# The search of the blocks' first edges in five groups, placed beside the adjacency blocks of a graph kernel

## What is computed

```
def spmm(x): return segment_sum(edge_weight[:, None] * x[src], dst, num_segments=n)
acc = cur = x
for _ in range(3):
    cur = spmm(cur); acc = acc + cur
x = layernorm(x + acc)

h = (x @ W_node.T).reshape(n, 4, 32);  e = (edge_attr @ W_edge.T).reshape(E, 4, 32)
att = leaky_relu(sum(concat[h[src], h[dst], e] * a), 0.2)
m = maximum(segment_max(att, dst), 0);  ex = exp(att - m[dst])
denom = segment_sum(ex, dst) + (E - deg) * exp(-m)
x = layernorm(x + segment_sum(ex / denom[dst] * h[src], dst))
```

## Time and profile before

| | |
|---|---|
| median of 3 runs | 1601.72 us (1601.37 to 1603.68) |
| the profiled execution | 1605.02 us, span 1603.3 us |
| PE busy | 1359.4 us, 85% |
| DVE busy | 1004.7 us, 63% |
| ACT busy | 681.5 us, 43% |
| 0 to 81 us | records, searches, counts; 24 attribute chunks |
| 82 to 413 us | the 25 adjacency blocks and 80 chunks |
| 431 to about 880 us | the three layers |
| to 1603 us | scores, attention, last norm |

### The profile page before, as it was taken

The page is one execution under the profiler, slowest core; times in us unless marked ns, Lnnn a source line. Parts: engine busy times, 40 slices in busy tenths (PEclk is TensorE's granted clock), DMA queues, the critical chain, the costliest instruction groups (busy, mean ns, idle before and its releaser), DMA issues.

```text
span 1603.3 us, 49688 instructions
## 1 busy us (share of the span) xinstructions
PE 1359.4 (85%) x22245; PEld 992.1 (62%) x22245; DVE 1004.7 (63%) x1519; ACT 681.5 (43%) x1600; POOL 130.5 (8%) x102
## 2 busy tenths in 40 slices
PE   4969999996499999999997898838888886888885
PEld 3959988886244454454445898825656654566564
DVE  5389999999200010000114898888888887888874
ACT  3236666664110000001111000047777777777776
POOL 1511011100000000000000000021111110111000
PEclk9999999998799999999997999968999998899998
DMA  6628787756779699869971776400000000000000
GB/s 207 222 82 242 220 248 218 233 150 160 229 258 409 228 345 325 300 215 373 301 281 44 201 208 202 136 29 13 13 13 13 13 13 8 12 13 14 26 3 24
DMA packets 214641, 250.30 MB, mean 156 GB/s; under 512 B 43578, under 2 KB 146487, under 8 KB 214294
## 3 DMA queue, kind: packets, MB, share of 16 engines
q1 hardware_dynamic: 210422, 236.52, 45.5%
q0 software_dynamic: 4000, 10.54, 2.1%
HBM read 197.88 MB, written 49.14 MB: 154 GB/s over the span
## 4 chain that ended last, share of the span: by engine, by line
PE 44%; DVE 27%; DVEq 12%; DMA 7%; issue 4%; ACT 4%; SPq 1%; POOL 0%; ACTq 0%; POOLq 0%
PE bank L682 25%; DVE Lq L1351 7%; DVEq L1304 5%; PE bank L609 4%; DVE L L1166 4%; DVE Hx L1358 3%; PE bank L749 3%; DVE Hw L1176 3%; PE bank L719 2%; DVEq L1366 2%; PE bank L579 2%; DVEq L1171 2%; DMA hib<-slp 2%; PE bank L760 2%; DMA drow<-in_dst,rowi 2%
## 5 line engine op out<-in xcount | busy, mean ns | idle before, releaser
L1014 ACT COPY Att<-bank 128x400 f32<-128x400 f32 x800 | 336.7, 525 | 121.7 <-PE bank L749 120.0
L749 PE MATMUL bank<-Hx,Lq 64*128 64x100 f16 x6400 | 229.7, 218 | 96.6 <-DVE Hx L1358 91.0
L749 PEld LDWEIGHTS bank<-Hx,Lq 64*128 64x128 f16 x6400 | 170.6, 100 | 176.8 <-DVE Hx L1358 103.6
L760 PE MATMUL bank<-Att,xa 128*32 128x128 f32 x5000 | 222.2, 295 | 0.0
L609 PE MATMUL bank<-L,Hw 128*52 128x128 bf16 x4800 | 167.9, 225 | 35.6 <-DVE Hw L1176 27.4
L1358 DVE TENSOR_TENSOR Hx<-Hq,wdup 128x3328 f16<-128x3328 f16 x100 | 184.7, 1889 | 3.7
L609 PEld LDWEIGHTS bank<-L,Hw 128*52 128x52 bf16 x4800 | 144.7, 108 | 45.4 <-DVE Hw L1176 38.8
L894 ACT COPY rows<-bank 116x512 f32<-116x512 f32 x200 | 117.8, 589 | 119.3 <-PE bank L609 105.1
L719 PE MATMUL bank<-Tp,lob 128*128 128x100 bf16 x2418 | 152.9, 211 | 15.9 <-DVE sel L1290 13.7
L719 PEld LDWEIGHTS bank<-Tp,lob 128*128 128x128 bf16 x2418 | 148.3, 99 | 19.7 <-DVE sel L1290 11.3
L682 PE MATMUL bank<-pieces,xs 128*128 128x512 f32 (+1 forms) x350 | 137.2, 552 | 17.8 <-DMA pieces<-adj 17.8
(11 more groups left out here) (175 smaller groups left out, 1359.1 us busy)
## 6 DMA issues: line engine op xcount, KB each, us to landing
pieces<-adj SPq DMA_DIRECT2D x90, 1280.0 KB, 8.9
adj<-rows SPq DMA_DIRECT2D x100, 416.0 KB
lob<-slp SPq DMA_DIRECT2D x26, 992.0 KB, 6.3
ea<-in_edge_attr SPq DMA_DIRECT2D x25, 992.0 KB, 8.5
hib<-slp SPq DMA_DIRECT2D x78, 64.0 KB, 4.8
pieces<-adj SPq DMA_DIRECT2D x15, 320.0 KB, 3.1
lh_d<-dup SPq DMA_DIRECT2D x25, 64.0 KB, 4.3
lhd<-lh_d SPq DMA_DIRECT2D x25, 64.0 KB, 1.8
```

The costliest lines, as they stand in the source:

```text
L749: m = pe.matmul(bank[i % 3 * 2 + d][:, v * H * NB:(v + 1) * H * NB].rearrange("p (h i) -> p h i", h=H), Lq[n % 2][rows, pp, :], Hx[n % 2][ ...
L760: m = pe.matmul(bank[7][h * HD:(h + 1) * HD, 0:P], xa[:, i, h * HD:(h + 1) * HD], Att[j % 2][:, h * NB + i, :], start=(i == 0), stop=(i == ...
L1014: m = act.copy(o[:, d, :, :], bank[i % 3 * 2 + d][:, 0:4 * H * NB].rearrange("p (q i) -> p i q", q=4))
```

## The change

- The searches, gathers and counts go in five groups of SGR = 5 blocks. `rows_found(g)` on DVE does the five searches of a group and converts them; `rows_of(g)` on POOL issues its five gathers; `starts_found(g)` on DVE does its five counts and their conversion.
- Group 0 is searched right after the edge checks and counted after the weight splits. The searches of groups 1 to 4 follow, then the flag. The counts of groups 1 to 4 stand in DVE's blocks, after the one-hots of blocks 0, 5, 10 and 15. POOL issues the gathers of the next group after the record gathers of blocks 2, 7, 12 and 17.
- On PE the product that spreads the first edges comes before those of the weights. On ACT its copy and the first cast of the weights come first.
- On SP the zero record and the records are stored before attribute group 1 and x are loaded.
- EPRE is 8 chunks instead of 24. The other 96 (and the two steps that trail behind) are in the blocks, four per block, now until the first half of block 24. The loads of attribute groups in the blocks move with them (`g = (j + 5) // 2`).
- `rows` has three buffers instead of two, and `L` three instead of four. The tiles of the search are kept through the blocks; the searches write into a tile of their own, `less_n`.

Left out below are the declarations that move, the semaphore name `adj2`, and the waits for all stores at the end of the blocks, which name three semaphores instead of two.

```diff
@@ -47,12 +47,12 @@
 NE = NG * NC
-EPRE = 3 * NC
+EPRE = NC
 EPB = 4
...
 RR = 3
-LB = 4
+LB = 3
 SETS = U // 4
@@ -62,7 +62,8 @@
 CUT = (0, 12, 24, 25)
-assert NE - EPRE == EPB * 20 and NPC * PC == NB
+SGR = 5
+assert NE - EPRE == EPB * 24 and NPC * PC == NB and NB == SGR * DR
 
...
@@ -133,7 +136,7 @@
                 dup, dupw = sb("dup", [P, 3, 2, U, 2], BF16, c), sb("dupw", [P, 3, U, 3, 2], BF16, c)
-                rows = [sb(f"rows{i}", [P, 8, BPB, P], F32, c) for i in range(2)]
+                rows = [sb(f"rows{i}", [P, 8, BPB, P], F32, c) for i in range(3)]
         with ExitStack() as c:
...
@@ -257,16 +260,16 @@
             load_attr(0)
-            load_attr(1)
             sp.wait_ge(s["consts"], 4)
-            sp.dma_start(xs[:, 0:NB - 1, :], x[0:(NB - 1) * P, :].rearrange("(b p) d -> p b d", p=P)).then_inc(s["ld_x"], 16)
-            for r0, r1 in ((0, 48), (48, NL)):
-                sp.dma_start(xs[r0:r1, NB - 1, :], x[(NB - 1) * P + r0:(NB - 1) * P + r1, :]).then_inc(s["ld_x"], 16)
             sp.dma_start(rec_d[P * RW:P * RW + U, :].rearrange("(o u) f -> o (u f)", o=1), zrec[0:1, :]).then_inc(s["rec_out"], 16)
...
                 .then_inc(s["rec_out"], 16)
+            load_attr(1)
+            sp.dma_start(xs[:, 0:NB - 1, :], x[0:(NB - 1) * P, :].rearrange("(b p) d -> p b d", p=P)).then_inc(s["ld_x"], 16)
+            for r0, r1 in ((0, 48), (48, NL)):
+                sp.dma_start(xs[r0:r1, NB - 1, :], x[(NB - 1) * P + r0:(NB - 1) * P + r1, :]).then_inc(s["ld_x"], 16)
             for g in range(2, EPRE // NC + 2):
@@ -281,7 +284,7 @@
                         store_dup(j + 2)
-                    g = (j + 9) // 2
+                    g = (j + 5) // 2
                     if j % 2 == 1 and EPRE // NC + 2 <= g < NG:
@@ -291,7 +294,7 @@
                             sp.dma_start(adj[j, d0:d0 + HP, :].rearrange("d (i n) -> i d n", n=P),
-                                         rows[j % 2][r0:r0 + HIP, :, :, :].rearrange("i o v n -> i (o v) n")).then_inc(s[f"adj{j % 2}"], 16)
+                                         rows[j % 3][r0:r0 + HIP, :, :, :].rearrange("i o v n -> i (o v) n")).then_inc(s[f"adj{j % 3}"], 16)
 
...
@@ -458,24 +461,32 @@
 
-            pool.wait_ge(s["rowi_ready"], 1)
             rows = dst.rearrange("(r w) -> r w", w=W1)
-            for j in range(NB):
-                if j >= DR:
-                    pool.wait_ge(s["dr_used"], j - DR + 1)
-                pool.indirect_dma_start(out=drow[:, j % DR, :], out_offset=None, in_=rows,
-                                        in_offset=bass.IndirectOffsetOnAxis(ap=rowi[:, j:j + 1], axis=0)).then_inc(s[f"dr{j % DR}"], 16)
+            def rows_of(g):
+                pool.wait_ge(s["rowi_ready"], g + 1)
+                for j in range(g * SGR, (g + 1) * SGR):
+                    if j >= DR:
+                        pool.wait_ge(s["dr_used"], j - DR + 1)
+                    pool.indirect_dma_start(out=drow[:, j % DR, :], out_offset=None, in_=rows,
+                                            in_offset=bass.IndirectOffsetOnAxis(ap=rowi[:, j:j + 1], axis=0)).then_inc(s[f"dr{j % DR}"], 16)
+            rows_of(0)
 
             def adjacency():
-                pool.wait_ge(s["off_ready"], 1)
                 pool.wait_ge(s["rec_out"], 32)
                 for j in range(NB):
+                    if j % SGR == 0:
+                        pool.wait_ge(s["off_ready"], j // SGR + 1)
                     if j >= RR:
...
                         .then_inc(s[f"recs{j % RR}"], 16)
+                    if j % SGR == 2 and j // SGR + 1 < NB // SGR:
+                        rows_of(j // SGR + 1)
 
...
@@ -545,14 +557,14 @@
             pe.wait_ge(s["consts"], 15)
+            pe.wait_ge(s["diag_ready"], 1)
+            pe.matmul(bank[3][:, 0:3 * P], ones[:, :], diag[:, :, :].rearrange("p k n -> p (k n)"), start=True, stop=True)\
+                .then_inc(s["fb_ps"], 1)
             pe.wait_ge(s["ld_wt"], 16 * (H + 3))
...
                       start=True, stop=True).then_inc(s["wt_ps"], 1)
-            pe.wait_ge(s["diag_ready"], 1)
-            pe.matmul(bank[3][:, 0:3 * P], ones[:, :], diag[:, :, :].rearrange("p k n -> p (k n)"), start=True, stop=True)\
-                .then_inc(s["fb_ps"], 1)
             pe.wait_ge(s["bad_sb"], 1)
@@ -827,6 +839,10 @@
         def _(act):
+            act.wait_ge(s["fb_ps"], 1)
+            act.copy(fbs[:, :], bank[3][:, 0:WR]).then_inc(s["fb_sb"], 1)
+            act.wait_ge(s["ld_w"], 48)
+            act.copy(rec[:, :, 2], w_r[:, :]).then_inc(s["wp1"], 1)
             act.wait_ge(s["wt_ps"], 1)
@@ -836,10 +852,6 @@
             act.nop().then_inc(s["wt_sb"], 1)
-            act.wait_ge(s["ld_w"], 48)
-            act.copy(rec[:, :, 2], w_r[:, :]).then_inc(s["wp1"], 1)
-            act.wait_ge(s["fb_ps"], 1)
-            act.copy(fbs[:, :], bank[3][:, 0:WR]).then_inc(s["fb_sb"], 1)
             act.wait_ge(s["wr1"], 1)
@@ -888,10 +900,10 @@
                 m = 4 * n + o
-                if hf == 0 and o == 0 and j >= 2:
-                    act.wait_ge(s[f"adj{j % 2}"], 64 * (j // 2))
+                if hf == 0 and o == 0 and j >= 3:
+                    act.wait_ge(s[f"adj{j % 3}"], 64 * (j // 3))
                 act.wait_ge(s["oct_ps"], m + 1)
-                act.copy(rows[j % 2][0:U + 2 * HIP, hf * 4 + o, :, :].rearrange("p v n -> p (v n)"), bank[m % 2][0:U + 2 * HIP, :])\
+                act.copy(rows[j % 3][0:U + 2 * HIP, hf * 4 + o, :, :].rearrange("p v n -> p (v n)"), bank[m % 2][0:U + 2 * HIP, :])\
                     .then_inc(s["oct_sb"], 1)
...
@@ -1097,6 +1109,30 @@
             dve.tensor_tensor(bad[:, 2:3], bad[:, 0:1], bad[:, 1:2], ALU.add).then_inc(s["bad_sb"], 1)
+            def rows_found(g):
+                bs = slice(g * SGR, (g + 1) * SGR)
+                for j in range(g * SGR, (g + 1) * SGR):
+                    dve.tensor_scalar(less_n[:, j % 2, 0:WR], fbs[:, :], dnode[:, j:j + 1], 0.0, ALU.is_lt, ALU.add, accum_out=nrow[:, j:j + 1])
+                    dve.drain()
+                dve.tensor_scalar(rowf[:, bs], nrow[:, bs], -1.0, 0.0, ALU.add, ALU.max)
+                dve.drain()
+                dve.tensor_copy(rowi[:, bs], rowf[:, bs]).then_inc(s["rowi_ready"], 1)
+            def starts_found(g):
+                bs = slice(g * SGR, (g + 1) * SGR)
+                for j in range(g * SGR, (g + 1) * SGR):
+                    dve.wait_ge(s[f"dr{j % DR}"], 16 * (j // DR + 1))
+                    dve.tensor_scalar(less_n[:, j % 2, :], i16(drow[:, j % DR, :]), dnode[:, j:j + 1], 0.0, ALU.is_lt, ALU.add,
+                                      accum_out=cnt[:, j:j + 1]).then_inc(s["dr_used"], 1)
+                    dve.drain()
+                dve.scalar_tensor_tensor(out=offf[:, bs], in0=rowf[:, bs], scalar=float(W1), in1=cnt[:, bs], op0=ALU.mult, op1=ALU.add)
+                dve.drain()
+                dve.tensor_copy(off[:, bs], offf[:, bs]).then_inc(s["off_ready"], 1)
+            dve.wait_ge(s["fb_sb"], 1)
+            rows_found(0)
             dve.wait_ge(s["wp1"], 1)
@@ -1107,25 +1143,13 @@
             dve.tensor_tensor(wt[:, 1, :], wt[:, 0, :], rec[:, :, 3], ALU.subtract).then_inc(s["wr2"], 1)
-            dve.wait_ge(s["fb_sb"], 1)
-            for j in range(NB):
-                dve.tensor_scalar(pj[:, j % 2, 0:WR], fbs[:, :], dnode[:, j:j + 1], 0.0, ALU.is_lt, ALU.add, accum_out=nrow[:, j:j + 1])
-                dve.drain()
-            dve.tensor_scalar(rowf[:, :], nrow[:, :], -1.0, 0.0, ALU.add, ALU.max)
-            dve.drain()
-            dve.tensor_copy(rowi[:, :], rowf[:, :]).then_inc(s["rowi_ready"], 1)
+            starts_found(0)
+            for g in range(1, NB // SGR):
+                rows_found(g)
             dve.wait_ge(s["bad_ps"], 1)
...
             dve.sem_inc(s["flag_ready"], 1)
-            for j in range(NB):
-                dve.wait_ge(s[f"dr{j % DR}"], 16 * (j // DR + 1))
-                dve.tensor_scalar(pj[:, j % 2, 0:W1], i16(drow[:, j % DR, :]), dnode[:, j:j + 1], 0.0, ALU.is_lt, ALU.add,
-                                  accum_out=cnt[:, j:j + 1]).then_inc(s["dr_used"], 1)
-                dve.drain()
-            dve.scalar_tensor_tensor(out=offf[:, :], in0=rowf[:, :], scalar=float(W1), in1=cnt[:, :], op0=ALU.mult, op1=ALU.add)
-            dve.drain()
-            dve.tensor_copy(off[:, :], offf[:, :]).then_inc(s["off_ready"], 1)
 
@@ -1179,7 +1203,6 @@
                 dve.wait_ge(s["rec_out"], 32)
-                dve.wait_ge(s["off_ready"], 1)
                 for i in range(2):
@@ -1194,10 +1217,12 @@
                     one_hots(2 * j + 1)
+                    if j % SGR == 0 and j // SGR + 1 < NB // SGR:
+                        starts_found(j // SGR + 1)
 
             def sources():
-                dve.wait_ge(s["adj0"], 64 * (NB - NB // 2))
-                dve.wait_ge(s["adj1"], 64 * (NB // 2))
+                for k in range(3):
+                    dve.wait_ge(s[f"adj{k}"], 64 * len(range(k, NB, 3)))
```

(22 more changed lines are left out.)

## The result

The changed kernel takes 1609.93 us in the median of 20 runs (1603.02 to 1621.68). The kernel before, on the same chips, takes 1603.8 us (1600.41 to 1609.58, 20 runs). The ratio is 1.0045 with a 95% interval of 1.0028 to 1.0061: slower by 6 to 7 us (the medians differ by 6.1), where 25 us less were forecast. The profiled execution of the changed kernel took 1606.84 us with a span of 1605.1 us, against 1605.02 and 1603.3.

A forecast was written before the change was run, and what follows sets the result against it. DVE was taken to set the pace in head and blocks. Terms -40.6 + 0.5 + 16.1 - 2.0 + 0.6 = -25.4 us took the profiled 1605.0 to 1579.6, or 1576.3 as a median; range 1571 to 1587.

The forecast's parts named there:

- The head, -40.6: Before the blocks: DVE starts them from 40.2 us instead of 80.80, first mask at 48.7; -40.6 us.
- rival B: Head: loads delay group 0's fifth gathered row, +5.1 us, and record gathers, +1.0 more: 1582 us; chance 0.10.
- Counts, +16.1: Blocks: counts of groups 1 to 4 on DVE, 4.02 us a group, no wait for rows; +16.1 us.
- Hidden, -2.0: Block 0 or 1: DVE's 2.0 us of waiting for PE vanishes behind the added counts; -2.0 us.
- rival C: Blocks: PE's clock drops in pauses behind counts; 0.7 us passed on in three places, +2.1: 1578 us; chance 0.12.
- From the last DVE product on, everything ... is the same work ... I carry it over unchanged: After the blocks: stores, layers, scores and attention are the same work in the same order, carried over unchanged.
- The 16 chunks moved cost nothing: Blocks: the 16 attribute chunks moved in from the head cost nothing while DVE sets the pace.
- Record gather +0.5: Start of the blocks: first record gathers, issued only after the flag, land at 48.3 to 49.9 us; +0.5 us.
- tail +0.6: Last block: chunks make PE's preceding half 2.8 us longer, so the last half ends later; +0.6 us.
- Buffers, 0: Blocks: one-hot buffers from four to three and a third buffer of finished rows change nothing; 0 us.
- Rival A: Blocks: 20 moved row gathers each hold DVE up by 0.95 us, 19 us more: 1595 us; chance 0.02.
- Rival D: Blocks: pauses leave PE slow for whole blocks, 9.7 us more each; four slow blocks give 1615 us; chance 0.04.

The follow-up runs named there:

- e8: Changed kernel with counts taken one by one behind the blocks and the blocks' attribute loads issued on ACT's queue: 1603.48 us, ratio 1.0015.
- e2: Changed kernel with the attribute loads among the blocks cut to 2 of 31 edge tiles: 1598.59 us, ratio 0.9978.
- e10: Changed kernel with counts of groups 2 to 4 one by one and one moved attribute group put back (16 chunks ahead of the blocks): 1607.12 us, ratio 1.0019.
- e9: Kernel before with the two buffer changes alone (three finished-row buffers, three one-hot buffers): 1602.47 us, ratio 0.9992.
- e5: Changed kernel with counts one by one behind the blocks and attribute loads among the blocks cut to 2 of 31 edge tiles: 1591.52 us, ratio 0.9935.
- e4: Changed kernel with the attribute loads of the blocks issued by ACT's queue instead of SP's: 1607.2 us, ratio 1.0034.
- e6: Changed kernel without the 20 counts of groups 1 to 4 in the blocks, row gathers, waits and conversions kept: 1602.86 us, ratio 1.0012.
- e11: As e10, with the attribute loads of the blocks issued by ACT's queue instead of SP's: 1606.18 us, ratio 1.0010.
- e12: The kernel of e1 without the 20 row gathers of groups 1 to 4 in the blocks: 1602.78 us, ratio 0.9993.
- e1: Changed kernel with counts of groups 2 to 4 taken one by one behind blocks 1 to 15: 1606.6 us, ratio 1.0041.
- e7: Kernel before with about 4 us of clearing an unused tile on DVE behind blocks 0, 5, 10 and 15: 1629.95 us, ratio 1.0170.
- e3: Kernel before with the attribute loads among the blocks cut to 2 of 31 edge tiles: 1602.95 us, ratio 1.0006.

## Why the prediction was wrong

By its own steps:

- **The head, -40.6.** Its order was right, the amount not: first mask at 54.49 instead of 48.7. That is near rival B's price of 5.1 + 1.0, in part by luck: the record gathers that were to make its 1.0 cost nothing. Its stated cause, a late fifth row, is the larger part (issued at 24.41 and used at 31.69, 7.3 us and not 3.2). The "0.95 a gather" was the other, 3.0 us until the fifth was issued: 0.95 is what a gather takes beside searches and counts; beside DVE's casts it is 1.4 to 2.65. I had the 1.56 of record gathers before me and used it only for the blocks. +5.8.
- **Counts, +16.1.** Right: 3.94 a group, no wait for rows.
- **Hidden, -2.0.** Wrong: DVE's waits for PE did not go, they rose to 12.6. This is rival C, and the term mis-sized was its slow spell. I took two slow octets with their chunks, 7.9 us, a half 3.7 us late of which 3.0 are swallowed: 0.7 in each of three places. Measured: 10 to 14 us of slow PE after each pause, a first half of 10.8 us and so 4.9 late, and 6.7 us of waits in the three places, not 2.1. The other 5.9 came behind an "issue" gap of PE that was in no rival. Against the forecast, +12.6.
- **"From the last DVE product on, everything ... is the same work ... I carry it over unchanged".** This step had no rival, and it is the one that failed most: +11.8, and with the pauses all but gone the same step takes nearly all of the gain (e8). The stores weren't on the list of what must keep pace. In the kernel before SP had 48.0 us of waiting for rows in the stage, 2 us in a block, and I never counted it. With two attribute groups and 20 gathers moved in, 23.5 were left. "The 16 chunks moved cost nothing" looked at DVE and PE only. That all loads among the stores together cost 11 us is shown (e2); that the two moved ones alone do is not, for e10 put one back and gained nothing.
- **Record gather +0.5, tail +0.6** are too small to be told apart in 406.06. **Buffers, 0**: right, by e9.
- **Rival A** didn't come: the first group of counts and the masks beside gathers keep their times. **Rival D** neither: no pause stuck.

The sum: forecast 1579.6 for the profiled execution, +5.8 +12.6 +11.8 = 1609.8; it took 1606.8. The 3 us left are 0.3 before PE's end and 2.8 behind the layers' start. No single rival led to the slower side; three costs on the same path did: the head, which B had; the waits for PE, of which C had a sixth; and the stores, which none had. Without P and T 11 us of gain are there, of some 19 (e5).

What stays open: by which mechanism transfers hold each other up. The share of the DMA engines stays at 0.71 to 0.78 in the stage, so they are not full by that measure; the rate is 201 to 206 GB/s in e4, e6, e8 and both kernels; and yet in e10, e11 and e12 it is 195, 199 and 196 (82 to 422 us), with fewer bytes and an end at best 2 us earlier (e12's layers at 432.62, e1's at 434.81), so it isn't a fixed budget of bytes. Shown is that full attribute loads beside the stores cost 11 to 15 us by the medians once the blocks start early (e2 against the changed kernel, e5 against e1), on SP's queue: about half of it before PE's last product (4.7 and 7.9 us), the rest behind it. That ACT's queue changes little is shown within the scatter (e4 against the changed kernel, e8 against e1: 3 us each by the medians).

None of the runs with all work left in is surely faster than the kernel before; e8 is equal to it.

## What to carry to other kernels

Before moving work from a head into a loop, make the budget of the loop for every queue as for every engine: the wait time that the store queue has left in a turn is the most that may be added, and the loop's end is where its last store lands. Work added to the engine that sets the pace costs more than its own length if it opens a pause on TensorE; one count of 0.72 us a block left pauses of 1.4 to 1.7 us, after most of which TensorE stayed fast, where 4 us at once cost a slow spell each time. A head that is shortened by x is a gain of x only if what it overlapped fits elsewhere.

## What the runs showed of the hardware

- Behind idle gaps of PE of 2.1 to 5.8 us among chunks and products its granted clock was 0.50 for 10 to 14 us (2.14, 2.67, 3.76 and 4.57 in the changed kernel, 4.86 to 5.84 in e7), with PE busy nearly all the time. In the kernel before, behind gaps of 4.20 and 4.34 us in blocks that have no chunks, it was 3.4 us each (369.1 to 372.5, 382.7 to 386.1). Of the 11 gaps of 1.4 to 1.7 us in e1 two had a slow spell behind them, of the 11 in e5 none, though a spell there stands behind a gap of 1.17 us (96.3 to 106.6). The spells don't all show in the recorded clock: in the changed kernel octets take up to 1.49 us from 64 to 75 too, and the window around them has 1.00:

```profile
60.00:80.00 20.00, 15.77 (x196) 14.76 (x196) 19.00 (x26) 6.71 (x14) 4.37 (x3) 1.00 0.07 19
```

- POOL's indirect gather of one row a partition took 0.95 us beside searches and counts, and 1.94, 2.65 and 1.41 us beside DVE's conversions and two-input operations (4.89 for the first one in e6 and e12), while these kept their time.
- The issue of the same store took a median 1.44 us on SP in one kernel and 2.41 us in the other. With light loads it was 1.25 (e3) and 1.68 (e2), and 0.86 in e9, where only buffers differ from the kernel before. So the issue time isn't a property of the transfer; what sets it isn't shown.
